# Late stretch of a two-layer graph kernel: one wait narrowed, one pass cut in two, weight parts made a pair step sooner

## The reference, cut to what matters

```python
edge_index = jnp.stack([src, dst])                       # 5000 edges, 10000 nodes, 512 features
x = x + gnn(layernorm(x), edge_index, edge_type, ...)    # two layers of:
#   w = einsum('rb,bio->rio', att, basis)                # 2 relations out of 30 bases
#   msg = sigmoid(x[col] @ gate_w[r]) * x[col] @ w[r]    # r is the edge's type
#   segment_sum(msg, row) + x @ root + bias              # relu between the layers
x = x + moe(layernorm(x))
#   shared = sum_n gelu(t @ sw1[n].T + sb1) @ sw2[n].T   # 2 shared experts of 64
#   routed = sum_e cw[e] * (gelu(t @ rw1[e].T + rb1) @ rw2[e].T + rb2)   # 8 experts, top 2
```

## Time and profile before

| | |
|---|---|
| median of 3 runs | 1632.76 us (1632.3 to 1637.3) |
| the profiled execution | 1634.88 us, of which the span from first to last instruction is 1633.2 us |
| PE busy | 1562.2 us, 96% of the span |
| DVE, ACT, POOL busy | 54%, 46%, 27% |
| DMA, mean over the span | 168 GB/s |
| mean granted TensorE clock | 0.986 of full |

### The profile page before, as it was taken

One profiled execution on the slowest core, in us unless ns is written; L12 is line 12 of the kernel. 1 busy time (PEld: TensorE's weight loads), 2 busy tenths in 40 slices (PEclk: granted clock), 3 DMA queues, 4 the chain that ended last, 5 costly groups with the idle time before them and its releaser, 6 DMA issues. The chain is left out here.

```text
span 1633.2 us, 24003 instructions
## 1 busy us (share of the span) xinstructions
PE 1562.2 (96%) x7903; PEld 1209.5 (74%) x7903; DVE 890.0 (54%) x2181; ACT 747.1 (46%) x1219; POOL 433.9 (27%) x570
## 2 busy tenths in 40 slices
PE   6999999989997999999999898999999999999998
PEld 4677666777785777677888776777777777777777
DVE  5555686867742333345665456555545554655553
ACT  3334334656641121123665436555555545554552
POOL 4762232467753000000567431011001100110000
PEclk9999999999998999999999998999999999999999
DMA  8999999487758999997777684333234323432201
GB/s 226 279 277 290 321 310 283 149 216 129 127 78 209 290 278 279 282 284 236 177 132 131 107 216 84 104 106 101 78 104 110 97 77 108 114 87 77 91 27 45
DMA packets 96838, 274.25 MB, mean 168 GB/s; under 512 B 13990, under 2 KB 14004, under 8 KB 89058
## 3 DMA queue, kind: packets, MB, share of 16 engines
q1 hardware_dynamic: 72498, 204.10, 40.8%
q0 software_dynamic: 24240, 68.93, 23.0%
HBM read 179.82 MB, written 92.76 MB: 167 GB/s over the span
## 5 line engine op out<-in xcount | busy, mean ns | idle before, releaser
L971 ACT ACTIVATE th<-bank 128x512 fp32r<-128x512 f32 x158 | 94.3, 598 | 300.9 <-PE bank L1219 286.4
L1199 PE MATMUL bank<-tth,w1h 128*128 128x512 f32 (+1 forms) x400 | 165.7, 414 | 3.4 <-ACT gel L1117 3.4
L1199 PE MATMUL bank<-w2h,gth 128*128 128x512 f32 x395 | 158.3, 401 | 0.8 <-DVE gtl L1740 0.8
L1199 PE MATMUL bank<-ttl,w1h 128*128 128x512 f32 (+1 forms) x400 | 157.4, 394 | 0.0
L1199 PE MATMUL bank<-tth,w1l 128*128 128x512 f32 (+1 forms) x400 | 156.3, 391 | 0.0
L1199 PE MATMUL bank<-w2l,gth 128*128 128x512 f32 x395 | 154.5, 391 | 0.0
L1199 PE MATMUL bank<-w2h,gtl 128*128 128x512 f32 x395 | 153.8, 389 | 0.0
L1504 DVE SCALAR_TENSOR_TENSOR tl<-bank,th 128x512 fp32r<-128x512 f32 x79 | 54.4, 691 | 170.1 <-ACT th L971 170.1
L1199 PE MATMUL bank<-root1h,th 128*128 128x512 f32 x316 | 133.1, 421 | 8.2 <-DVE yout L1533 6.6
L1199 PE MATMUL bank<-root2h,th 128*128 128x512 f32 x316 | 133.5, 423 | 6.9 <-DVE tl L1504 3.8
L1199 PE MATMUL bank<-root1l,th 128*128 128x512 f32 x316 | 126.5, 400 | 0.0
(11 more groups left out here) (212 smaller groups left out, 3642.0 us busy)
## 6 DMA issues: line engine op xcount, KB each, us to landing
basis_t<-in_gnn_basis SPq DMA_DIRECT2D x64, 896.0 KB
xin<-in_x SPq DMA_DIRECT2D x39, 512.0 KB, 8.2
xin<-y SPq DMA_DIRECT2D x39, 512.0 KB, 5.1
zr<-in_x SPq DMA_DIRECT2D x19, 1024.0 KB, 5.0
out<-zr SPq DMA_DIRECT2D x19, 1024.0 KB, 3.9
y<-yout SPq DMA_DIRECT2D x37, 512.0 KB
zr<-z POOLq DMA_DIRECT2D x18, 1024.0 KB, 8.0
z<-yout SPq DMA_DIRECT2D x34, 512.0 KB
```

Of the source, the lines that this page charges most:

```text
L971: act.activation(th_a[:, s, :], tpb[s][:], f).then_inc(s_hi, 1)
L1199: ins = pe.matmul(out_ap, a(k), b(k), start=first, stop=last)
```

## The change

Five edits. Pair 38 is given the buffer yout 1 in place of yout 0. ACT's `gelu(0,0)` waits only for the add of pair 34 (whose buffer `gel` lies on) and `g_hi(0,0)` for that of pair 37; DVE waits for `s_late2[1]` and `s_late2[2]` alone, and POOL's wait for all late adds goes behind its read of z for group 3. `add_first` and the moments of group 0 are done in two halves each: the first half of `add_first` in step 6 and the second in step 7 (where all of it was), the first half of the moments in step 8 (where all of them were) and the second in step 9, behind `y_out` of step 8. The moments of group 1 go behind the router of group 0. The first five weight parts are made in pair steps 15 to 19 and no longer in 16 to 20.

```diff
         def late2_buffer(g):
-            k = (g - NC // 2) % 4
+            k = (0, 1, 2, 3, 1)[g - NC // 2]
         def late2_added(eng):
             for k in range(5):
-                eng.wait_ge(s_late2[k], 16 * (len(LATE2_PAIRS[k::4]) if k < 4 else 1))
+                eng.wait_ge(s_late2[k], 32 if k == 1 else 16)
         def z_added(eng, q):
-                eng.wait_ge(s_zx, 1)
+                eng.wait_ge(s_zx, 2)
# gpsimd
             def group(q):
+                if q.i is None and q.k == 1:
+                    late2_added(pool)
...
             group_rstd(Pos(1))
-            late2_added(pool)
             walk_groups(pool, group)
# scalar
-                if phase == SD and u >= NPAIR - 5:
-                    expert_hi(u - (NPAIR - 5))
+                if phase == SD and NPAIR - 6 <= u < NPAIR - 1:
+                    expert_hi(u - (NPAIR - 6))
...
-            late2_added(act)
+            act.wait_ge(s_late2[0], 16)
             gelu(Pos(0), 0)
+            act.wait_ge(s_late2[3], 16)
             g_hi(Pos(0), 0)
# vector
                 if st.phase == SE and st.g.k - 4 in LATE2_PAIRS and not apart:
-                    dve.wait_ge(s_late2[0], 16)
+                    dve.wait_ge(s_late2[1], 16)
...
-                if phase == SD and u >= NPAIR - 5:
-                    expert_lo(u - (NPAIR - 5))
+                if phase == SD and NPAIR - 6 <= u < NPAIR - 1:
+                    expert_lo(u - (NPAIR - 6))
...
                 if i == LAST_E - 2:
-                    q_stats(Pos(0), range(QT), True)
+                    q_stats(Pos(0), range(0, 2), False)
+                if i == LAST_E - 1:
+                    q_stats(Pos(0), range(2, QT), True)
                 y_out(st)
                 if i < FC:
                     expert_lo(FC + i)
+                elif i == LAST_E - 4:
+                    add_first(range(0, 2))
                 elif i == LAST_E - 3:
-                    add_first()
+                    add_first(range(2, QT))
...
-            q_stats(Pos(1), range(QT), True)
             chain, _ = steps(Pos(0), ROUTER)
             route_a(Pos(0), chain)
             route_b(Pos(0), chain)
+            q_stats(Pos(1), range(QT), True)
             bias_rows()
-            late2_added(dve)
+            dve.wait_ge(s_late2[1], 32)
+            dve.wait_ge(s_late2[2], 16)
```

More of the change, by code:

```diff
@@ L1818, in group, with add_first @@
                     q_out(q, j)
-            def add_first():
+            def add_first(js):
                 dve.wait_ge(s_zin[0], 16)
                 dve.wait_ge(s_z0, 16)
-                for j in range(QT):
+                for j in js:
                     ins = dve.tensor_tensor(zr[:, 0, j, :], zr[:, 0, j, :], z0[:, j, :], ALU.add)
```

## The result

| | before | after |
|---|---|---|
| median of 22 runs each | 1633.54 us | 1637.62 us |
| ratio, with its 95% interval | | 1.0029 [1.0017, 1.0040] |
| the profiled execution | 1634.88 us, span 1633.2 | 1636.30 us, span 1634.7 |
| mean granted clock | 0.986 | 0.988 |

By the ratio the changed kernel is slower by 0.29%, 4.7 us, with an interval that leaves out no change (the two medians differ by 4.1 us). The forecast was 3.9 us more.

A forecast was written before the change was run, and what follows sets the result against it. PE is busy 96% of the span, so only its idle or lower-clock time between 930 and 1014 us can be won. Terms 5.7 - 2.6 + 0.8 = +3.9 us on 1632.76 give 1636.7 us, range 1632.0 to 1640.5.

The forecast's parts named there:

- first term: At group 0's moments and `tn`: DVE's `y_out` of step 8 waits for pair 35's add; +5.7 us.
- second term: From `tn` of group 0 to `tfull` of group 1: narrowed gelu wait and router ahead of group 1's moments; -2.6 us.
- The early part: Start of the late steps: `tl` of step 0 comes 1.8 us sooner, late steps 3.3 us sooner at best.
- POOL 2.55 us: POOL's steps behind group 1's moments were costed at 2.55 us, as before, ending at 993.95.
- PE's wait for `tn` of group 1: Near 1000 us, behind chunk 2 of the up products, PE stands about 2.9 us.
- Third term: Last stretch, chunk 3 on PE partly at the lower clock: +0.8 us, bounds 0 and 1.9.
- the second: Rival: pair 35 lands by 967.3, end moves by -4.4 us to 1628.4; terms cancel from 971.3; chance 0.13.
- Slower by more: Rival: a DMA issued by POOL lands 3 us later, delaying gth or gtl; 1639.7 us; chance 0.13.
- The wait was not hidden: Denies the rival that the added wait is hidden and group 0 starts where it did; 1632 to 1634; chance 0.08.

The follow-up runs named there:

- e7: The kernel before with only the first five weight parts made a pair step sooner; ratio to before 1.0013.
- e6: The kernel before with only pair 38 moved to yout 1, waiting for pair 35's add in place of pair 34's; ratio to before 0.9981.
- c1: The changed kernel with DVE's four bias rows moved ahead of the router, right behind the late steps; ratio to before 1.0023.
- e2: The changed kernel with the moments of group 1 put back ahead of the router of group 0; ratio to before 0.9978.
- e1: The changed kernel with pair 38 in a buffer of its own, so y_out of step 8 waits for no add; ratio to before 0.9991.
- e5: The changed kernel with SP's x loads of groups 2 and 3 held until pair 35's add has landed; ratio to before 1.0000.
- e8: The kernel before with ACT's and DVE's waits narrowed and pair 38 in a buffer of its own, nothing else changed; ratio to before 0.9960.

## Why the prediction was right

It gave 1636.7, range 1632.0 to 1640.5, and named the mechanism. By its terms, each as the difference of the two kernels' traces, the first pair and the repeats:

| stretch | predicted | first pair | repeats |
|---|---|---|---|
| POOL's first late add to `tn` of group 0 | +5.7 | 22.38 - 17.85 = +4.5 | 22.32 - 17.42 = +4.9 |
| from there to `tfull` of group 1 | -2.6 | 24.27 - 25.71 = -1.4 | 24.76 - 25.56 = -0.8 |
| from there to the end | +0.8 | 633.65 - 632.58 = +1.1 | 633.73 - 632.64 = +1.1 |
| sum | +3.9 | +4.2 | +5.2 |

- **The sum owes something to luck.** The first term's loss was put 0.8 to 1.2 us too high and the second term's gain 1.2 to 1.8 us too high, and the two errors cancel in large part.
- **The early part**: right. PE's first wait is 1.8 us shorter, and e7 has the 3.3 us at best. That the scatters do not feel it was right as well. The two microseconds that `add_first` was to lose waiting for `z0` hang on the scatters' end: 1.90 us in the second trace, none in the first.
- **First term**: right in its place, about 1 us too large. The forecast had `yout` 17.8 us behind POOL's first add; it came at 16.9 and 16.8. The landing took 16.2 us where 16.8 was taken from before. DVE's idle time was 6.1 and 6.6, forecast 7.5, and PE's wait for `tl` of step 10 4.75 and 5.25, forecast 6.7. The price hangs as much on when DVE arrives (31.2 and 33.5 us behind T0, forecast 32.6) as on the landing: in e6, where it came at 37.3, the same add held it 0.63 us.
- **Second term**: mis-sized, -2.6 against -1.4 and -0.8. The router took the forecast 4.45 us. "POOL 2.55 us" failed: its three lines took 3.78, because the moments were moved to where the bias rows run beside POOL (c1, without them, 2.75). The 2.55 was read at the old place, beside the router's small instructions. `tn` of group 1 came 20.1 and 20.6 us behind that of group 0, forecast 19.1.
- The same term put two edits into one sum. Its own numbers had POOL done with group 1 at 988.7 before the move and 993.95 behind it; that 5.3 us was set against gelu's wait and counted as part of a gain. e2 shows it as a loss.
- **PE's wait for `tn` of group 1**: forecast 2.9, measured 5.64 and, in the repeat, 4.10. In the first trace 1.0 us is the lateness of that `tn`, and the other 1.7 is PE being earlier, since its first up products ran at the full level (984.0 to 991.3). In the repeat they did not, the wait is 1.5 us shorter, and the tail is the same within 0.5 us: how early PE arrives has no part in the end.
- **Third term**: +1.1, within 0 to 1.9, and by the forecast's mechanism: chunk 3 begins at the lower level (0.62 from 1001.0 to 1007.4), and PE then no longer waits for the last hidden part. The last chunk of the first down product begins 60.5 and 61.0 us behind POOL's first add, 56.3 before; in the time of before that is 1017.6 and 1018.1, forecast 1016.5 to 1018.5. This term is all that the clock costs behind `tfull` of group 1; in e1 (a wait of 3.47 us) and e2 (none) the stretch is back at 632.8 and 632.6 us.
- **The rivals**: the second had the terms cancel from a landing 3.5 us sooner on. In e5, where loads were held back, `yout` came 13.6 us behind POOL's first add where the forecast had 17.8, and the kernel came out at no change, as that rival says. "Slower by more", by a late DMA behind POOL, did not happen: neither ACT nor PE waits for an add behind 972. The wait was not hidden.

## What to carry to other kernels

Value each edit of a bundle against leaving it out, not against the kernel before: here narrowed waits worth about 5 us in e8's trace were overspent by two moves of about 6 us each, of which one looked free because what it delayed had been hidden by the very wait that was taken away. When half of a piece of work is put behind an instruction that waits for a DMA, ask how early the engine will now arrive there. A duration read at the old place of an instruction is not that of the new one if another engine's neighbours change.

## What the runs showed of the hardware

- A chain of 21 dependent pairs of indirect scatter-adds ended 19.2 to 23.2 us behind a fixed point of the program, in 14 traces, with no visible relation to the edits; single traces of a kernel that hangs on such a chain are best compared from its end.
- Two small POOL instructions slowed beside DVE's 128x512 ones with two SBUF inputs: the 128x4 one from 1.04 to 1.46 us, the four of 128x1 from 0.97 to 1.83.
- An accumulating add of 512 KB into HBM, the second of two, landed 16.2 us behind its issue beside the x and z loads, and 13.0 with two x loads of 1 MB held back.
